# Attention scores of a round's two query blocks issued together, ahead of all four mask products

## The chip, the cores and the metric

The kernel runs on one NeuronCore of a Trainium2 chip. The metric is the device time of one execution in microseconds, lower is better.

## What is computed

Causal self-attention with rotary embedding (2 sequences of 1024 tokens, 1024 channels, 32 heads of 32), a post-norm, a gated feed-forward layer whose weights are looked up in a codebook, and a second post-norm. The part that the change touches is this:

```python
scores = jnp.einsum('bnth,bnsh->bnts', q, k) * (1.0 / math.sqrt(h))
causal = jnp.tril(jnp.ones((T, T), dtype=bool))
scores = jnp.where(causal, scores, -jnp.inf)
attn = jax.nn.softmax(scores, axis=-1)
out = jnp.einsum('bnts,bnsh->bnth', attn, v)
```

## The kernel before

Each engine has its own program, written out by hand in the order in which it runs; semaphores join them. Attention is done in 16 passes (8 groups of 4 heads, 2 sequences) of 8 rounds, 128 rounds in all. A round `u` handles two heads and two query blocks of 128 rows: a short one (`o` = 0) and a long one (`o` = 1), out of the list (0,7), (1,6), (2,5), (3,4), taken in turn. Block number t sees t+1 key blocks, so the two together always have 9, and a short block has 128 to 512 keys and a long one 1024 down to 640. Below, "the (2,5) round" is a round of the third kind.

Rounds are pipelined three deep. In round `u` TensorE (`attention_round`) does, in this order:

1. `scores(i, u, 0)`: the short block's scores for the two heads. The contraction is over 32 rows, so each head's product uses a strip of 32 rows of the array, and the two heads' strips run side by side. Float32 products are recorded as two passes each. Then two mask products (L321 before the change) over all 128 rows: the identity times the triangular mask, in bfloat16, added to the diagonal 128 columns in PSUM. Each raises `scores_done`.
2. `scores(i, u, 1)`: the same for the long block, with keys from 512 on computed in two further strips from the copy `qk_far` (the rows that read `big`), and two mask products.
3. `turn(i, u-1, ...)` (L334): transposes of the previous round's probabilities, in six groups `j` = 0 to 5 (short block: 0 and 1; long block: 2, 3 for the first head, 4, 5 for the second). They alternate between PSUM banks 6 and 7, so group `j` waits until ScalarE has copied out group `j`-2 (`turns_copied`).
4. Between groups 3 and 4, `weigh(i, u-2)` (L353): probabilities times values of the round before that.

`scores(i, u, 0)` waits for the previous round's second exponential and for `o_copied`, the last copy of `weigh(i, u-3)`'s outcome; `scores(i, u, 1)` waits for the previous round's fourth exponential (`exp_done`), since it overwrites the PSUM banks that this one reads.

VectorE in a round: `row_max` 0 and 1 (L922, the maxima of the short block, waiting for `scores_done`), `normalise(u-1, 3)` (L927 reciprocal, L929 scaling), `normalise` 0, `row_max` 2, `normalise` 1, `row_max` 3, two output copies (L937), `normalise` 2.

ScalarE in a round: exponentials 0 and 1 (L629, waiting for the maxima), the copies of turned groups 0 to 3 of the previous round (L638), exponentials 2 and 3, copies 4 and 5. After every fourth round it also issues two loads of queries and keys (L611, L617).

Of the kernel before, what the change touches and what calls it, by code (L numbers as in the profile page):

```python
# [16 lines left out]
P = 128  # L17
# [24 lines left out]
def round_of(u):  # L42

    p, k = divmod(u % ROUNDS, len(BLOCKS))
    return (2 * p, 2 * p + 1), BLOCKS[k]
# [35 lines left out]
def seq_post_ln_layer(nc, x_nat, xT, wqT, wkT, wvT, woT, codebook, entries, idx, codes, cos, sin, ident,  # L81
                      mask, kp, hi_row, sel, out):
    ctx = ExitStack()
    with ctx:
# [186 lines left out]
        def _(pe):  # L271
# [29 lines left out]
            def scores(i, u, o):  # L301

                heads, tbs = round_of(u)
                tb = tbs[o]
                bank, wide, L, d0 = 4 - 4 * o, 1 + o, (tb + 1) * P, tb * P
                if u % 4 == 0:
                    pe.wait_ge((qk_in, far_in)[o][heads[0] // 2], i * 16 + (u // ROUNDS * 16 + 16))
                if not (isinstance(i, int) and i * ROUNDS + u == 0):
                    pe.wait_ge(exp_done, i * STEPS + (4 * u - 2 + 2 * o))
                if o == 0 and not (isinstance(i, int) and i * ROUNDS + u < 3):  # L310
                    pe.wait_ge(o_copied, i * (2 * ROUNDS) + (2 * u - 4))
                for c0 in range(0, L, N):
                    w = min(N, L - c0)
                    for n, hh in enumerate(heads):
                        strip = hh if c0 == 0 else (hh + 2) % HG
                        r = slice(strip * HD, (strip + 1) * HD)
                        qk = qk_sb if c0 == 0 else qk_far
                        mm(ps[:, bank + wide * n + c0 // N, 0:w], qk[r, 0, d0:L], qk[r, 1, c0:c0 + w],
                           start=True, stop=(c0 + w < L))
                for n in range(2):  # L320
                    mm(ps[:, bank + wide * n + d0 // N, d0 % N:d0 % N + P], idb_sb, mask_sb,  # L321
                       start=False, stop=True).then_inc(scores_done, 1)

            def turn(i, u, o, heads=(0, 1)):
                tb = round_of(u)[1][o]
                for n in heads:
                    for c in range(1 + o):
                        j = o * (2 + 2 * n) + (1 - o) * n + c
                        if c == 0:
                            pe.wait_ge(probs_ready, i * STEPS + (4 * u + 2 * o + n + 1))  # L330
                        if not (isinstance(i, int) and i * ROUNDS + u == 0 and j < 2):
                            pe.wait_ge(turns_copied, i * (TURNS * ROUNDS) + (TURNS * u + j - 1))
                        for s in range(4 * c, min(4 * c + 4, tb + 1)):
                            last = nc.tensor.transpose(ps[:, 6 + j % 2, (s % 4) * P:(s % 4 + 1) * P],  # L334
                                                       probs_of[u % 2][2 * o + n][:, s * P:(s + 1) * P], id_sb[:, :])
                        last.then_inc(turns_done, 1)

            def weigh(i, u, free):


                heads, tbs = round_of(u)
                if u % 4 == 0:
                    pe.wait_ge(v_in[heads[0] // 2], i * 16 + (u // ROUNDS * 16 + 16))
                if free:
                    pe.wait_ge(exp_done, i * STEPS + (4 * (u + 2) + 2))
                pe.wait_ge(turns_copied, i * (TURNS * ROUNDS) + (TURNS * u + 6))
                for s in range(tbs[1] + 1):
                    for o in range(2):
                        for n, hh in enumerate(heads):
                            if s <= tbs[o]:  # L350
                                rhs = long_turned[:, u % 2, n, s, :] if o else short_turned[:, u % 2, n, s, :]
                                strip = (hh + 2 * o) % HG
                                last = mm(ps[strip * HD:(strip + 1) * HD, 4 + o, 0:P],  # L353
                                          v_sb[:, hh // 2, s, (hh % 2) * HD:(hh % 2 + 1) * HD], rhs,
                                          start=(s == 0), stop=(s == tbs[o]))
                        if s == tbs[o]:
                            last.then_inc(pv_done, 1)

            def attention_round(i, u, weighed=True, turned=True):

                scores(i, u, 0)
                scores(i, u, 1)
                if turned:
                    turn(i, u - 1, 0)
                    turn(i, u - 1, 1, (0,))
                if weighed:
                    weigh(i, u - 2, True)
                if turned:
                    turn(i, u - 1, 1, (1,))
# [10 lines left out]
            for u in range(2):  # L380
                attention_round(0, u, False, u > 0)
            with pe.Fori(0, PASSES - 1) as i:
                pe.sem_inc(pe_passed, 1)
                for u in range(2, ROUNDS + 2):
                    attention_round(i, u)
            for u in range(2, ROUNDS):
                attention_round(PASSES - 1, u)
# [777 lines left out]
```

## Time and profile before

| | |
|---|---|
| median of 3 runs | 6752.01 us (6750.79 to 6754.25) |
| the profiled execution, own time | 6752.44 us |
| its span (first to last instruction) | 6750.5 us |
| TensorE busy / VectorE / ScalarE / GpSimd | 6615.4 / 4662.0 / 3789.6 / 4927.0 us |
| mean granted TensorE clock | 0.996 of full speed |

The attention rounds fill the stretch from about 680 to 1530 us; before it are the projections, after it the output projection and the feed-forward layer. The profile names engines PE (TensorE products), PEld (its weight loads), DVE (VectorE), ACT (ScalarE), POOL (GpSimd). "L334" is a line of the kernel. Ends of TensorE's products are modelled by the profiler, so distances on TensorE are read below from start to start.

### The profile page before, as it was taken

What the parts mean: (1) busy time and instruction counts of PE and PEld (TensorE: products, weight loads), DVE (VectorE), ACT (ScalarE), POOL (GpSimd) and SP (SyncE); (2) the same over time, 40 slices, a digit from 0 to 9 for tenths busy, and PEclk for the clock granted to TensorE, in tenths of its full rate; (3) what the DMA queues carried; (4) which work ended last, traced back from release to release, by engine and by line L of the source; (5) the groups of instructions that cost most, each with busy time, mean ns of one, the idle gap of its engine ahead of it and who ended that gap; (6) DMA issues with size and microseconds to landing.
All of it is one profiled execution on the core that took longest, in us unless ns stands there. A gap on an engine that the chain in (4) does not pass through costs nothing.

```text
span 6750.5 us, 115830 instructions
## 1 busy us (share of the span) xinstructions
PE 6615.4 (98%) x29584; PEld 4063.9 (60%) x29584; DVE 4662.0 (69%) x11407; ACT 3789.6 (56%) x6692; POOL 4927.0 (73%) x5188
## 2 busy tenths in 40 slices
PE   9999899999999999999999999999999999999998
PEld 3444566666666666666666666666666666666664
DVE  3320888886776876777667776777767777677764
ACT  0000788886666755556555555555556555555552
POOL 7777777777777777777777777777777777777772
PEclk9999999999999999999999999999999999999999
DMA  4232232233333333333333333333333333333331
GB/s 140 64 90 48 56 60 55 58 80 75 82 84 74 78 72 75 65 74 73 73 68 74 76 74 73 67 74 74 72 75 67 73 73 74 74 66 73 73 71 63
DMA packets 479940, 490.59 MB, mean 73 GB/s; under 512 B 228672, under 2 KB 349248, under 8 KB 472896
## 3 DMA queue, kind: packets, MB, share of 16 engines
q10 hardware_dynamic: 298720, 425.47, 22.5%
q0 software_dynamic: 165888, 21.57, 7.8%
q1 hardware_dynamic: 14688, 36.48, 1.4%
q8 instruction: 220, 3.60, 0.2%
q14 instruction: 424, 3.47, 0.2%
HBM read 426.34 MB, written 56.72 MB: 72 GB/s over the span
## 4 chain that ended last, share of the span: by engine, by line
PE 75%; ACT 1%; issue 1%; DVE 0%; DMA 0%; ACTq 0%; DVEq 0%
PE ps L427 42%; PE ps L457 18%; PE ps L476 9%; PE ps L402 3%; PE ps L438 3%; PE ps L444 1%; ACT onehot L771 0%; ACT onehot L775 0%; PE ps L413 0%; PE ps L557 0%; DVE small L1068 0%; ACT arena L866 0%; DMA out_dram<-arena 0%; DVE onehot L1018 0%; DMA arena<-code_low 0%
## 5 line engine op out<-in xcount | busy, mean ns | idle before, releaser
L216 POOL DMA_INDIRECT raw<-in_codebook_dram,idx_sb x5184 | 4926.8, 950 | 1720.6 <-DMA raw<-in_codebook_dram,idx_sb 1566.8
L1018 DVE TENSOR_SCALAR_CACHE_REDUCE onehot<-arena,small 128x512 fp32r<-128x512 f32 x3845 | 2623.4, 743 | 1049.0 <-PE ps L427 998.8
L427 PE MATMUL ps<-onehot,table 128*128 128x512 f32 x12288 | 3267.6, 417 | 23.0 <-ACT onehot L775 18.7
L427 PEld LDWEIGHTS ps<-onehot,table 128*128 128x128 f32 x12288 | 2290.7, 188 | 900.1 <-issue 353.9
L771 ACT ACTIVATE onehot<-arena,small 128x512 fp32r<-128x512 f32 x2307 | 1496.7, 713 | 1139.1 <-PE ps L427 980.1
L775 ACT ACTIVATE onehot<-onehot,small 128x512 fp32r<-128x512 f32 x2307 | 1487.4, 708 | 0.0
L457 PE MATMUL ps<-big,arena 128*128 128x512 f32 x2752 | 1267.9, 597 | 0.0
L457 PEld LDWEIGHTS ps<-big,arena 128*128 128x128 f32 x2752 | 510.2, 189 | 571.7 <-issue 543.7
L1025 DVE SCALAR_TENSOR_TENSOR picked<-arena,small,ps 128x512 f32<-128x512 f16 x768 | 572.3, 745 | 158.3 <-PE ps L438 142.2
L476 PE MATMUL ps<-arena 128*128 128x512 f32 (+1 forms) x1408 | 640.4, 600 | 1.8 <-ACT arena L744 1.2
L922 DVE TENSOR_REDUCE small<-ps 128x1 f32<-128x384 f32 (+7 forms) x512 | 374.2, 752 | 270.1 <-PE ps L321 267.5
L1010 DVE TENSOR_TENSOR big<-ps,big 128x512 f32<-128x512 f32 x704 | 484.9, 691 | 109.8 <-PE ps L476 100.1
L284 PE MATMUL ps<-big,arena 128*128 128x512 f32 x1024 | 442.2, 595 | 16.6 <-DMA big<-in_xT_dram 16.6
L629 ACT ACTIVATE arena<-ps,small 128x384 f32<-128x384 f32 (+7 forms) x512 | 378.1, 745 | 85.9 <-DVE small L922 79.2
L476 PEld LDWEIGHTS ps<-arena 128*128 128x128 f32 (+1 forms) x1408 | 249.0, 190 | 279.8 <-issue 255.1
L334 PE MATMUL ps<-id_sb,arena 128*128 128x128 f32 x2304 | 331.3, 280 | 51.2 <-ACT arena L638 49.4
L638 ACT COPY arena<-ps 128x512 f32<-128x512 f32 (+3 forms) x768 | 330.6, 485 | 65.9 <-PE ps L334 63.8
L284 PEld LDWEIGHTS ps<-big,arena 128*128 128x128 f32 x1024 | 195.4, 191 | 262.6 <-issue 262.6
L1018 DVE DVE_READ_ACCUMULATOR onehot<-arena,small 128x1 f32 x3845 | 321.2, 84 | 0.0
L753 ACT ACTIVATE arena<-ps 128x512 f32<-128x512 f32 (+1 forms) x88 | 52.5, 597 | 467.9 <-PE ps L457 465.1
L334 PEld LDWEIGHTS ps<-id_sb,arena 128*128 128x128 f32 x2304 | 246.6, 141 | 109.2 <-ACT arena L638 74.5
L929 DVE TENSOR_SCALAR arena<-arena,small 128x384 f32<-128x384 f32 (+7 forms) x512 | 276.4, 540 | 18.1
(74 smaller groups left out, 2726.1 us busy)
## 6 DMA issues: line engine op xcount, KB each, us to landing
arena<-code_low ACTq DMA_DIRECT2D x770, 256.0 KB
arena<-code_high ACTq DMA_DIRECT2D x770, 128.0 KB
raw<-in_codebook_dram,idx_sb POOLq DMA_INDIRECT x5184
gathered_units<-raw SPq DMA_DIRECT2D x39, 512.0 KB
arena<-gathered_units ACTq DMA_DIRECT2D x19, 1024.0 KB
queries_keys<-arena ACTq DMA_DIRECT2D x16, 1024.0 KB, 4.0
arena<-queries_keys ACTq DMA_DIRECT2D x32, 512.0 KB
big<-queries_keys ACTq DMA_DIRECT2D x32, 512.0 KB
```

The source lines that it names most:

```text
L216: pool.indirect_dma_start(raw[:, s, n, :], None, codebook, bass.IndirectOffsetOnAxis(ap=idx_sb[:, s, n:n + 1], axis=0), engine_sem=describ ...
L284: last = mm(ps[:, 4 * m + 2 * b + h, :], w_sb[:, m, k, :], big1[:, k, b * T + h * N:b * T + (h + 1) * N], start=(k == 0), stop=(k == KT - 1))
L334: last = nc.tensor.transpose(ps[:, 6 + j % 2, (s % 4) * P:(s % 4 + 1) * P], probs_of[u % 2][2 * o + n][:, s * P:(s + 1) * P], id_sb[:, :])
L427: last = mm(ps[:, 4 + s % 2, :], table[:, k, c, :], onehot[:, k, :], start=(k == 0 and c == 0), stop=(k == KLO - 1 and c == PIECES - 1))
L457: one = mm(ps[:, 2 * (t % 2) + m, :], w_rep[:, m, k, :], big1[:, k, t * N:(t + 1) * N], start=(k == 0), stop=(k == CS - 1))
L476: mm(ps[:, d % banks, :], d_rep[rows, h * P:(h + 1) * P], hT[rows, t * N:(t + 1) * N], start=True, stop=True).then_inc(down_done, 1)
L629: act.activation(probs_of[u % 2][e][:, 0:L], src[:, 0:L], ACT.Exp, bias=negmax[:, e:e + 1], scale=1.0, accum_out=rowsum[:, e:e + 1]).then_ ...
L771: act.activation(onehot[:, k, :], lo_sb[:, s % 2, :], ACT.Abs, bias=kp_sb[:, k:k + 1], scale=-1.0).then_inc(distance_done, 1)
L775: act.activation(onehot[:, k, :], onehot[:, k, :].bitcast(F32), ACT.Relu, bias=one_sb, scale=-1.0).then_inc(near_ready, 1)
L1010: dve.tensor_tensor(big2[:, h, cols], ps[:, d % banks, :], before[:, h, cols], ALU.add).then_inc(y_added, 1)
L1018: dve.tensor_scalar(onehot[:, k, :], lo_sb[:, s % 2, :], kp_sb[:, k:k + 1], None, ALU.is_equal, ALU.add, accum_out=hits[:, k:k + 1]).then_ ...
L1025: dve.scalar_tensor_tensor(picked[:, s % QUAD, :], hi_sb[:, s % 4, :], hi_row_sb, ps[:, 4 + s % 2, :], ALU.is_equal, ALU.mult).then_inc(ma ...
```

## The change

The mask products move out of `scores` into a function of their own, which is called twice after both calls of `scores`.

```diff
                         mm(ps[:, bank + wide * n + c0 // N, 0:w], qk[r, 0, d0:L], qk[r, 1, c0:c0 + w],
                            start=True, stop=(c0 + w < L))
+
+            def mask_diagonal(u, o):
+                d0 = round_of(u)[1][o] * P
+                bank, wide = 4 - 4 * o, 1 + o
                 for n in range(2):
                     mm(ps[:, bank + wide * n + d0 // N, d0 % N:d0 % N + P], idb_sb, mask_sb,
                        start=False, stop=True).then_inc(scores_done, 1)
@@
                 scores(i, u, 0)
                 scores(i, u, 1)
+                mask_diagonal(u, 0)
+                mask_diagonal(u, 1)
                 if turned:
                     turn(i, u - 1, 0)
                     turn(i, u - 1, 1, (0,))
```

No other engine's program changes. TensorE's rows at the head of a (2,5) round, before; L318 are the scores (the short block has 384 keys), L321 the mask products, L334 the transposes:

```order
L311 REGISTER_ALU [waits exp_done]
L318 MATMUL ps<-arena 128x384 [waits o_copied]
L318 MATMUL ps<-arena 128x384
L321 MATMUL ps<-arena 128x128 x2
L309 REGISTER_ALU
L318 MATMUL ps<-arena 128x512 [waits exp_done]
L318 MATMUL ps<-arena 128x512
L318 MATMUL ps<-big 128x256 x2
L321 MATMUL ps<-arena 128x128 x2
L330 REGISTER_ALU
L332 ISA [waits probs_ready]
L334 MATMUL ps<-id_sb,arena 128x128 [waits turns_copied]
```

The same place after the change, where the mask products stand on L325 and the transposes on L338:

```order
L311 REGISTER_ALU [waits exp_done]
L318 MATMUL ps<-arena 128x384 [waits o_copied]
L318 MATMUL ps<-arena 128x384
L309 REGISTER_ALU
L318 MATMUL ps<-arena 128x512 [waits exp_done]
L318 MATMUL ps<-arena 128x512
L318 MATMUL ps<-big 128x256 x2
L325 MATMUL ps<-arena 128x128 x4
L334 REGISTER_ALU
L336 ISA [waits probs_ready]
L338 MATMUL ps<-id_sb,arena 128x128 [waits turns_copied]
```

The short block's two mask products now stand behind the long block's wait for `exp_done` and behind its four score products.

## Rows read from the trace of the kernel before

**Rows 1.** Busy time by stretch: us, busy us (instructions) of PE, PEld, DVE, ACT, POOL, clock, DMA.

```profile
680.00:1530.00 850.00, 786.88 (x8870) 518.96 (x8870) 738.12 (x1786) 701.10 (x1785) 634.47 (x647) 0.99 0.30 61
1530.00:6750.00 5220.00, 5166.50 (x19179) 3252.07 (x19178) 3756.34 (x9437) 3071.07 (x4891) 3787.48 (x4011) 1.00 0.32 73
```

**Rows 2.** The line of the scores: durations in ns, first and last start in us.

```profile
L318 PEld LDWEIGHTS ps<-arena x1024: 181/184/333, 679.9 to 1524.1; 32*128 32x128 f32 x171
```

**Rows 3.** Waits from 680 to 1530 us: total us, times, longest us.

```profile
PEld ps L321 <- issue: 149.9, 224, 1.5
ACT arena L629 <- DVE small L922: 79.2, 104, 5.2
PEld ps L334 <- ACT arena L638: 74.5, 120, 0.9
...
PE ps L334 <- ACT arena L638: 48.2, 125, 0.8
```

**Rows 4.** Timeline of PE, a (2,5) round: start us, us, instruction, count, [idle before].

```profile
1015.72 0.91 PE L318 MATMUL ps<-arena 32*128 32x384 f32 x4 [0.28 <-DVE big L937]
1016.56 0.28 PE L321 MATMUL ps<-arena 128*128 128x128 bf16 x2
1016.78 0.70 PE L318 MATMUL ps<-arena 32*128 32x512 f32 x2
...
1017.84 0.29 PE L321 MATMUL ps<-arena 128*128 128x128 bf16 x2
1017.96 0.61 PE L334 MATMUL ps<-id_sb,arena 128*128 128x128 f32 x4
1018.97 0.98 PE L334 MATMUL ps<-id_sb,arena 128*128 128x128 f32 x7 [0.41 <-ACT arena L638]
```

**Rows 5.** Timeline of DVE, then of ACT, in the same round.

```profile
1016.83 1.02 DVE L922 TENSOR_REDUCE small<-ps 128x1 f32<-128x384 f32 x2 [0.25 <-PE ps L321]
...
1017.42 0.58 ACT L629 ACTIVATE arena<-ps,small 128x384 f32<-128x384 f32 x1 [0.31 <-DVE small L922]
...
1017.99 0.57 ACT L629 ACTIVATE arena<-ps,small 128x384 f32<-128x384 f32 x1
...
1018.55 0.64 ACT L638 COPY arena<-ps 128x256 f32<-128x256 f32 x2
```

**Rows 6.** Timeline of PE, a (0,7) round and the start of the (1,6) round.

```profile
1003.42 0.49 PE L318 MATMUL ps<-arena 32*128 32x128 f32 x4
1003.84 0.28 PE L321 MATMUL ps<-arena 128*128 128x128 bf16 x2
...
1009.43 0.70 PE L318 MATMUL ps<-arena 32*128 32x256 f32 x4
1010.06 0.29 PE L321 MATMUL ps<-arena 128*128 128x128 bf16 x2
```

**Rows 7.** Timeline of ACT in the (0,7) round; ACTq is its queue issuing DMAs.

```profile
1004.22 0.56 ACTq L617 DMA_DIRECT2D big<-queries_keys  x1
1004.90 0.37 ACT L629 ACTIVATE arena<-ps,small 128x128 f32<-128x128 f32 x1 [0.73 <-DVE small L922]
...
1005.89 1.08 ACT L638 COPY arena<-ps 128x512 f32<-128x512 f32 x2 [0.19 <-PE ps L334]
...
1008.97 1.12 ACT L629 ACTIVATE arena<-ps,small 128x1024 f32<-128x1024 f32 x1
1009.97 0.22 ACT L629 ACTIVATION_READ_ACCUMULATOR arena<-ps,small 128x1 f32 x1
```

**Rows 8.** Timeline of DVE in the (0,7) round.

```profile
1004.70 0.60 DVE L929 TENSOR_SCALAR arena<-arena,small 128x640 f32<-128x640 f32 x1
1005.39 0.16 DVE L927 RECIPROCAL small<-small 128x1 f32<-128x1 f32 x1
...
1007.32 1.22 DVE L922 TENSOR_REDUCE small<-ps 128x1 f32<-128x1024 f32 x1
1008.57 0.68 DVE L937 COPY big<-ps 64x128 f32 x2
```

## The prediction, made before the changed kernel ran

> **What bounds the kernel now.** I read the busy time by stretch first. The change touches only the attention stretch; behind it TensorE is busy 5166.5 of 5220 us [rows 1], so nothing there can absorb time that attention loses or pass on more than it gains. In attention TensorE is busy 786.9 of 850 us, VectorE 738.1 and ScalarE 701.1 [rows 1]: three engines close together, so the busy share settles nothing and the waits must. The scores start at 679.9 and last at 1524.1 us [rows 2]; over 127 steps that is 6.65 us a round.
>
> The table of waits [rows 3] shows where TensorE stands still: the transposes (L334) wait for ScalarE's copies (L638), 74.5 us on the load and 48.2 us on the product, some 125 times each, so about once a round. ScalarE's exponentials in turn wait for VectorE's maxima (79.2 us), and these for the mask products. That is a chain that crosses all three engines once a round. One (2,5) round shows it link by link [rows 4, 5]:
>
> - 1016.56 first mask product of the short block
> - 1016.83 VectorE starts the maxima (0.27 later, the product's latency)
> - 1017.42 ScalarE's exponential 0, after 0.31 us of standing idle for the maxima
> - 1017.99 exponential 1
> - 1018.55 copy of turned group 0, with no idle time before it
> - 1018.97 TensorE's group 2, after 0.41 us of idle time
>
> The reader is to see that from the mask product to group 2 there is no slack: each link starts when the one before it is done, and TensorE, at the far end, waits. All the rest of the round (group 3, `weigh`, groups 4 and 5, the next scores) stands behind group 2. So what sets the round is when the short block's mask products are done, and that is what the change postpones.
>
> **The price of the change on TensorE alone.** From the first pass of the short scores to the mask product it is 0.42 us with 128 keys, 0.63 with 256, 0.84 with 384 [rows 4, 6]: 0.21 for each 128 keys and a fixed 0.21. I read the fixed part as the first weight load and the wait for the strips to run empty before the mask product's 128 rows are taken up. From the mask product to the long scores it is 0.22, from the long scores to their mask products 1.06, from there to the first transpose 0.12 for two mask products [rows 4]. Today a (2,5) round takes 2.24 us from 1015.72 to 1017.96. Without the mask products in between, the long scores' passes follow the short ones on the same strips, as second passes follow first ones today, so the fixed 0.21 is hidden: 0.63 (short) + 1.06 (long) + 0.12 + 0.12 (four mask products) = 1.93 to 1.95, about 0.30 less. Over 128 rounds that is 38 us of TensorE's time.
>
> The trace shows a cost at each change between strips and the whole array: the mask products' loads waited 149.9 us, 224 times [rows 3], though most of that is the long streaming itself. The Trainium skill says the same as a rule (TensorEngine Tiling (Array Packing), Key Properties: changing the tiling mode drains TensorE). By that rule alone the change removes one such pair per round and is a gain of the 38 us above; by the chain the gain is not on the path. Both are weighed among the rivals.
>
> **The price on the chain.** The short block's first mask product moves from "short scores + 0.21 + its streaming" to "streaming + 1.06": later by 1.06 - 0.21 = 0.85 us. Bounds: if nothing of the fixed 0.21 is hidden, 1.06; it can't be under 0.85, since the long scores stream for that long. I take 0.85, because a second pass on a strip is what the long scores are like. Behind the moved products are queued VectorE's maxima 0 and 1, and everything that VectorE has behind these; in its program `normalise` stands behind them and can't go ahead. The long block's maxima don't notice: VectorE reaches them about 2 us later than the first ones.
>
> (2,5) and (3,4) rounds, 64 in all, have the pattern of [rows 4, 5]: the whole 0.85 us arrives at group 2. +0.85 each. That transposes 0 and 1 come 0.30 earlier only makes TensorE's wait longer, by 1.15.
>
> (0,7) rounds are different in two ways. ScalarE's exponential 0 is late anyway, because of the loads it issues until 1004.78, and copy 0 waits for the transposes (0.19) [rows 7]. With the maxima starting at 1003.84 + 0.85 + 0.27 = 1004.96, exponential 0 starts at about 1005.29, exponential 1 and copy 0 0.36 later each: 1006.01 against 1005.89, only +0.12. But VectorE then becomes the bound. It had 0.18 us to spare before `normalise` 0 (the scaling that starts at 1004.70 is over, by pace, at 1005.21 and the next starts at 1005.39) [rows 8] and runs without a gap from there to maximum 3 and the output copies. So these come 0.85 - 0.18 = 0.67 later: maximum 3 ends at 1009.20 instead of 1008.53, exponential 3 starts at about 1009.24 instead of 1008.97 (+0.27) [rows 7]. Output copies: 0.67 later, less 0.18 that the second one waits for `weigh` today, plus its time: it ends at about 1009.74, and the next short scores, which need it, start at 1009.77 instead of 1009.43 (+0.34) [rows 6].
>
> (1,6) rounds then meet the wait that the change puts in front of the mask products: the long scores may not start before exponential 3 of the round before is read out. It is read out at 1009.97 + 0.22 = 1010.19 now [rows 7], hence at 1010.46, and the scores can go at 1010.50, though the strips are free at 1009.77 + 0.42 = 1010.19. The mask product comes at 1010.50 + 1.06 = 1011.56 instead of 1010.06 [rows 6]: +1.50 for the (0,7) and (1,6) rounds together. In the other rounds exponential 3 is long done when the strips are free (its round's order is the same, and the short scores stream 0.42 to 0.85 us), so the wait costs nothing there.
>
> **Sum.** 1.50 + 0.85 + 0.85 = 3.20 us for four rounds. 127 rounds have transposes behind the scores, 31.75 times four: 101.6 us. Against the profiled execution, 6752.44 + 101.6 = 6854.0 us. The median of the runs, 6752.01, is 0.4 us from that execution, which makes no difference.
>
> **Bounds.** Low: VectorE and the exponential don't bind in the first two kinds, 0.12 + 3 x 0.85 = 2.67, which is 85 us (6837). High: nothing of the fixed 0.21 is hidden, so 0.21 more in (2,5), in (3,4) and once in the first two: 3.83, which is 122 us (6874). With a few us for the ends: 6832 to 6878.
>
> **The rivals.**
>
> 1. TensorE is the bound, as its busy share says, and the drain saved per round is what counts: 38 us less, 6714 us, faster. For it: 787 of 850 us busy. Against it: TensorE waits for ScalarE about once a round, 0.41 us in [rows 4], and the path that ends that wait has no idle time of its own. It decides from the point where the path from the first mask product to group 2 has more than 0.85 us to spare; today it has none. Chance 0.04.
>
> 2. The copies wait for the transposes in all rounds, as copy 0 does in the (0,7) round [rows 7], rather than for the exponentials. Then each round pays only 0.12 and the sum is 4 x 0.12 x 31.75 = 15 us, 6768 us. Against it: no idle time before copy 0 in the (2,5) round [rows 5]. Chance 0.04, of which 0.02 within the limit of "same".
>
> 3. The new wait binds in all rounds, not in one of four: exponential 3, then the long scores, mask products, maxima, exponentials, copies and exponential 3 again is a closed loop. If each round pays as the (1,6) round does, 1.50 - 0.34 = 1.16, the sum is 4 x 1.16 x 31.75 = 147 us, 6900 us. For it: three engines at over 80%. Against it: the exponential of a (0,7) round is the longest (1024 keys) and the short scores behind it are nearly the shortest. Chance 0.08.
>
> That the change doesn't do what it says I rule out: TensorE's rows stand in the program in the new order in every round.
>
> **How the numbers follow.** My forecast, with its bounds, 0.84; rival 1 0.04; rival 2 0.04; rival 3 0.08. The predicted time is the forecast's, 6854 us. The range from 6832 to 6878 leaves out the three rivals. About 0.2% (13.5 us) is what a measurement of this kernel can tell from no change: faster 0.04, same 0.02, slower 0.94.
>
> **What would show it.** Right: the attention stretch about 100 us longer and the stretches around it as long as before; TensorE busy in it no more than before, with its waits for ScalarE's copies more than doubled (some 1 us a round more); VectorE's first maxima waiting for the mask products in every round; the step from one round's first scores to the next's longer by about 0.34, 1.16, 0.85 and 0.85 us from (0,7) to (3,4). Wrong, toward rival 1: the same waits as today and a stretch of about 806 us. Wrong, toward rival 3: the long scores waiting for the exponential in all rounds.

## The result and the profile after

The changed kernel takes 6887.3 us (median of 6 runs, 6877.6 to 6895.1) against 6754.3 us for the kernel before (6 runs beside it): a ratio of 1.0198, 95% interval 1.0186 to 1.0209, or 133 us more. The forecast was 102 us more, 6854 us in a range from 6832 to 6878. So the sign and three quarters of the size came out, and the time lies above the range. The profiled execution took 6895.1 us with a span of 6893.3 us, 142.8 us over the span before.

First where the time went. Busy time by stretch of the changed kernel, with the columns of [rows 1]; the last three figures are the granted clock, the DMA share and GB/s:

```profile
680.00:1673.00 993.00, 796.16 (x8832) 550.12 (x8833) 734.63 (x1782) 696.85 (x1780) 736.16 (x750) 0.94 0.27 53
1673.00:6893.00 5220.00, 5166.98 (x19221) 3256.56 (x19220) 3758.32 (x9441) 3073.07 (x4897) 3690.69 (x3909) 1.00 0.32 73
```

What follows attention is as long as before: a stretch of 5220 us holds 5167.0 us of TensorE's work against 5166.5 [rows 1], and from the last round's first scores to the end it is 5226.6 us against 5227.8. The attention stretch has grown from 850 to 993 us, all of the difference. In it VectorE and ScalarE do the work of before; TensorE's is 9 us more, and its granted clock has gone from 0.99 to 0.94. The prediction has no term for that.

The waits between 680 and 1673 us, to be laid beside [rows 3]:

```profile
DVE small L928 <- PE ps L325: 391.4, 127, 226.7
...
PEld ps L338 <- ACT arena L644: 188.6, 120, 2.0
ACT arena L635 <- DVE small L928: 186.1, 137, 11.4
PE ps L338 <- ACT arena L644: 166.6, 125, 1.8
PEld ps L325 <- issue: 98.8, 128, 1.5
```

The first row is VectorE's maxima waiting for the mask products, once a round (226.7 us of it is one wait ahead of the first round). TensorE's waits for ScalarE's copies have gone from 74.5 and 48.2 us to 188.6 and 166.6 us, still about once a round; the one wait of the mask products' loads is left where there were two. The timeline of PE shows a (2,5) round and the (3,4) round after it, the counterpart of [rows 4]:

```profile
890.74 0.92 PE L318 MATMUL ps<-arena 32*128 32x384 f32 x4 [0.19 <-DVE big L943]
...
892.44 0.40 PE L325 MATMUL ps<-arena 128*128 128x128 bf16 x4
892.68 0.61 PE L338 MATMUL ps<-id_sb,arena 128*128 128x128 f32 x4
894.85 0.98 PE L338 MATMUL ps<-id_sb,arena 128*128 128x128 f32 x7 [1.57 <-ACT arena L644]
895.77 1.95 PE L357 MATMUL ps<-arena 128*32 128x128 f32 x36
...
898.56 0.70 PE L318 MATMUL ps<-arena 32*128 32x512 f32 x2
...
900.48 0.40 PE L325 MATMUL ps<-arena 128*128 128x128 bf16 x4
...
903.34 1.54 PE L338 MATMUL ps<-id_sb,arena 128*128 128x128 f32 x6 [1.80 <-ACT arena L644]
904.81 2.62 PE L357 MATMUL ps<-arena 128*32 128x128 f32 x36
...
908.17 0.38 PE L318 MATMUL ps<-arena 32*128 32x128 f32 x2
```

From the first scores to the mask products of the (2,5) round it is 1.70 us where it was 0.84: 0.86 later, forecast 0.85. From the first scores to the first transpose it is 1.94 us where it was 2.24: the 0.30 us that TensorE saves is there too, and stands as idle time (1.57 us instead of 0.41) in front of the next transposes. The step from this round to the next is 7.82 us, 0.86 more than the 6.96 us before (1015.72 to 1022.68, where the next round's first scores stand).

The (3,4) round is something else. Its six transposes after the wait take 1.54 us and its 36 products 2.62 us, where the kernel before needs 0.87 and 1.74 for the same:

```profile
1022.68 1.13 PE L318 MATMUL ps<-arena 32*128 32x512 f32 x4
...
1026.61 0.87 PE L334 MATMUL ps<-id_sb,arena 128*128 128x128 f32 x6 [0.64 <-ACT arena L638]
1027.41 1.74 PE L353 MATMUL ps<-arena 128*32 128x128 f32 x36
```

The busy time of the changed kernel in that stretch, with the granted clock as the third figure from the end:

```profile
903.40:906.80 3.40, 3.40 (x34) 2.86 (x36) 2.26 (x5) 2.58 (x7) 2.48 (x4) 0.52 0.06 3
```

TensorE stood idle for 1.80 us, and as it takes up work again it runs at the lower of its two levels, 1.2 GHz, for 3.4 us; that makes this round's step 9.61 us instead of 8.05. The Trainium skill (TensorE: Matmul & The Clock Gate, Terms) gives the penalty of such a stretch as half of its length, which makes an estimate of 1.7 us here. The trace agrees roughly: the two entries are 0.67 and 0.88 us longer, 1.55 together.

Read over the whole trace, 25 of the steps between rounds from the second round on are such slow ones (22 after (3,4), 3 after (2,5) rounds). One of the three is not a fall after a wait: it begins at 704.2 us, in the low stretch at the start of attention, which ends at 708.7 us here and at 697.5 us in the kernel before. The 25 are 39 us longer in all than quick steps of the same kind. The quick steps average 6.50, 7.15, 7.82 and 8.05 us from (0,7) on, against 6.01, 6.12, 6.97 and 7.20 before: 3.22 us more in four rounds, forecast 3.20. 31.75 times 3.22 is 102 us, and 102 + 39 = 141 of the 142.8 us between the spans.

### The profile page after: what moved, and what is told of

Same layout as the page of the kernel before. It is cut to its first block, busy times and chain, and to the rows that moved or that the text cites. A ratio compares the mean times of both kernels' runs of the same rounds, so it can differ in the third digit from the quotient of the medians.

```text
span 6893.3 us, 115830 instructions
## 1 busy us (share of the span) xinstructions
PE 6625.6 (96%) x29584; PEld 4100.0 (59%) x29584; DVE 4660.4 (68%) x11407; ACT 3787.4 (55%) x6692; POOL 4933.0 (72%) x5188
## 4 chain that ended last, share of the span: by engine, by line
PE 74%; ACT 1%; issue 1%; DVE 0%; DMA 0%; ACTq 0%; DVEq 0%
PE ps L433 41%; PE ps L463 17%; PE ps L482 9%; PE ps L408 3%; PE ps L444 3%; PE ps L450 1%; ACT onehot L777 0%; PE ps L419 0%; ACT onehot L781 0%; PE ps L563 0%; DVE small L1074 0%; DVE onehot L1024 0%; ACT arena L872 0%; DMA out_dram<-arena 0%; DMA arena<-code_low 0%
## 5 line engine op out<-in xcount | busy, mean ns | idle before, releaser
L1031 DVE SCALAR_TENSOR_TENSOR picked<-arena,small,ps 128x512 f32<-128x512 f16 x768 | 572.2, 745 | 157.8 <-PE ps L444 142.8
L338 PE MATMUL ps<-id_sb,arena 128*128 128x128 f32 x2304 | 346.6, 289 | 171.6 <-ACT arena L644 167.8
L338 PEld LDWEIGHTS ps<-id_sb,arena 128*128 128x128 f32 x2304 | 257.5, 146 | 230.3 <-ACT arena L644 188.6
```

The lines of the kernel that those rows point to most:

```text
L1031: dve.scalar_tensor_tensor(picked[:, s % QUAD, :], hi_sb[:, s % 4, :], hi_row_sb, ps[:, 4 + s % 2, :], ALU.is_equal, ALU.mult).then_inc(ma ...
```

## The experiments

Two theories stood against each other. **Chain and clock**: the chain over VectorE and ScalarE costs 3.2 us in four rounds as forecast, and the longer waits also cost TensorE its clock. **Chain alone, mis-sized**: the missing 31 us are a dearer chain. A "fall" below is a fall of the granted clock to the lower level. Steps given below for an experiment are read from the starts in its timeline, in the steady part of attention.

### The change in two kinds of rounds only

```diff
                 scores(i, u, 0)
+                if u % 4 in (0, 1):
+                    mask_diagonal(u, 0)
                 scores(i, u, 1)
-                mask_diagonal(u, 0)
+                if u % 4 not in (0, 1):
+                    mask_diagonal(u, 0)
                 mask_diagonal(u, 1)
```

This is e1_late_kinds; e2_early_kinds has (2, 3) in both places.

> The changed order is used in the (2,5) and (3,4) rounds only; the other two kinds keep the order of before. Theory (chain price as in the prediction, plus TensorE clock falls to half speed after the long waits): the chain costs 0.85 us in each of 64 rounds, 54 us over before; on top of it some clock falls of about 1.6 us each in the (3,4) rounds, between 0 and 30 us in all, since these rounds keep their wait of 2 us. So 6808 to 6840 us. Rival (the 33 us missing in the prediction were a mis-sized chain price in these two kinds): the rounds without a fall of the clock take over 7.9 and 8.2 us instead of 7.82 and 8.05.

> The changed order is used in the (0,7) and (1,6) rounds only. Theory: +1.50 us for each pair of them (0.34 and 1.16), 32 pairs, 48 us over before, hence 6802 us, and no falls of the clock in the middle of the attention rounds, because the waits that remain are 1.6 us and less. Rival (the chain price of this pair is mis-sized): more than 6815 or less than 6790 us with the clock at full speed.

Measured: e1 6849.5 us (4 runs) and e2 6796.1 us (4 runs) against 6751.3 us (13 runs): ratios 1.0147 (1.0130 to 1.0164) and 1.0067 (1.0050 to 1.0084), or 98 and 45 us more. Busy time from 720 to 1500 us, of e1 and then of e2:

```profile
720.00:1500.00 780.00, 675.81 (x7459) 465.26 (x7457) 618.13 (x1489) 584.67 (x1490) 582.50 (x596) 0.95 0.27 52
```

```profile
720.00:1500.00 780.00, 684.68 (x7877) 456.76 (x7874) 645.58 (x1579) 617.71 (x1580) 580.42 (x590) 1.00 0.28 55
```

e2, the clock at 1.00, is the chain price of the first two kinds by itself: steps of 6.39 and 7.15 us, 1.41 together over before, forecast 1.50; 32 pairs make 45 us, which is what was measured. That the two agree to the microsecond is luck: in this trace it is 50 us more from the first round to the last, a longer stretch at the low clock at the start included, and 6 us less behind them. (What follows the last round's start takes 5221 to 5228 us in these traces, e4's apart.) e1's quick steps are 7.83 and 8.06 us, 0.86 each over before, as forecast, and its clock is at 0.95. It has 26 slow steps (18 in the (3,4) and 8 in the (2,5) rounds), 42 us in all, so 54 + 42 = 96 of the 98 us. The theory's form held, but I had given the falls 0 to 30 us, and the time lies above the expected range: there are as many as in the changed kernel, though half of the rounds keep their short waits. So how often the clock falls can't be summed from the kinds: 98 + 45 is 143, and the changed kernel pays 133.

### The wait filled with work

```diff
+                        if j == 1:
+                            for _ in range((10, 12, 15, 0)[u % 4]):
+                                nc.tensor.transpose(ps[:, 7, 0:P], id_sb[:, :], id_sb[:, :])
                         for s in range(4 * c, min(4 * c + 4, tb + 1)):
```

> The changed kernel, with 10, 12 and 15 extra transposes of the identity (about 0.11 us each) ahead of transpose group 1 in the (1,6), (2,5) and (3,4) rounds, where TensorE stands waiting for ScalarE's copy anyway; their outcome is overwritten by group 1. Theory: they cost nothing on the chain, keep TensorE at work, and the granted clock stays at full speed from the second pass on; what is left is the chain price of 102 us, 6854 to 6862 us, 25 to 33 us faster than the changed kernel. Rival (the missing 33 us are chain, not clock): 6887 us or more, as TensorE's extra work can only lengthen a chain.

Measured: 6855.0 us (4 runs), ratio to before 1.0154 (1.0137 to 1.0170). That is 104 us over the kernel before beside it, where the changed kernel is 133 us over its own: 29 us less, though TensorE has 1184 transposes more to do. The timeline of PE in a (3,4) round; L339 are the added transposes:

```profile
1010.67 0.40 PE L325 MATMUL ps<-arena 128*128 128x128 bf16 x4
1010.90 0.50 PE L341 MATMUL ps<-id_sb,arena 128*128 128x128 f32 x3
1011.24 1.80 PE L339 MATMUL ps<-id_sb 128*128 128x128 f32 x15
...
1013.53 0.88 PE L341 MATMUL ps<-id_sb,arena 128*128 128x128 f32 x6 [0.17 <-ACT arena L647]
1014.34 1.74 PE L360 MATMUL ps<-arena 128*32 128x128 f32 x36
```

and its busy time from 720 to 1500 us:

```profile
720.00:1500.00 780.00, 730.76 (x8348) 537.71 (x8345) 608.76 (x1476) 579.25 (x1477) 579.70 (x592) 1.00 0.27 52
```

Group 2 starts 2.86 us after the mask products, as in the changed kernel (900.48 to 903.34), so the chain is untouched; the wait before it is 0.17 us, the transposes are back at 0.88 and the products at 1.74, the clock at 1.00, and no step is slow past the first rounds. 6855 us is the forecast's 6854: what the forecast lacked is the clock. (That the two agree to the microsecond is chance: the steps are 6.56, 7.16, 7.83 and 8.06 us, 3.3 us more in four rounds, and in this trace it is 107 us more from the first round to the last and 6 us less behind them.) "Chain alone" has fallen.

### The wait of one kind filled

```diff
-                            for _ in range((10, 12, 15, 0)[u % 4]):
+                            for _ in range((0, 0, 15, 0)[u % 4]):
```

> The changed kernel with the 15 extra transposes in the wait of the (3,4) rounds only; (1,6) and (2,5) rounds keep their waits of 1.6 and 1.8 us. Theory: most falls of the clock came at the end of the (3,4) rounds' wait of 2.07 us (19 of 27 such rounds in the profile against 1 of 27 for (2,5)); with that wait filled nearly all of them are gone, 6855 to 6865 us. Rival (the clock falls for the waits of all rounds taken together, whichever is filled): some falls move to the (2,5) rounds, and the time lies between 6865 and 6887 us.

> The kernel of e7_fill_34_only again, beside runs of before without the stalls. The profile of e7 had no slow (3,4) round but nine falls of the clock in its steady part. If a fall belongs to the (3,4) rounds' wait: 6853 to 6860 us. If falls move to the (2,5) rounds once the (3,4) rounds are filled: 6862 to 6882 us, with 7 to 18 slow (2,5) rounds in the profile.

These runs, and e5, e6, e8, e9, e10 and e13, fell on three chips on which the kernel before itself took 13,210 us: engines stood for thousands of us without a cause that the profile shows, before attention and in its first 18 rounds or so, while the other rounds run undisturbed. In every one of these traces the disturbed rounds end within some 20 us of GpSimd's last gather (7252 to 7261 us), so the undisturbed ones run without gathers beside them. The kernel before was not profiled there. So only differences count here, and above all the steps of the undisturbed rounds. Measured: 110 us over before both times, ratios 1.0084 (1.0068 to 1.0099) and 1.0082 (1.0067 to 1.0098). The timeline of PE of e11, a (2,5) and a (3,4) round:

```profile
7607.27 0.61 PE L341 MATMUL ps<-id_sb,arena 128*128 128x128 f32 x4
7609.44 1.55 PE L341 MATMUL ps<-id_sb,arena 128*128 128x128 f32 x7 [1.57 <-ACT arena L647]
7610.92 3.00 PE L360 MATMUL ps<-arena 128*32 128x128 f32 x36
...
7617.25 1.80 PE L339 MATMUL ps<-id_sb 128*128 128x128 f32 x15
...
7619.55 0.88 PE L341 MATMUL ps<-id_sb,arena 128*128 128x128 f32 x6 [0.17 <-ACT arena L647]
```

No (3,4) round is slow any more, and eight (2,5) rounds are (nine in e7), after a wait of 1.57 us that in the changed kernel cost nothing except twice. The rival was right: the falls moved. In the last 108 rounds, the undisturbed ones, the changed kernel has 20 falls, so filling one kind took away rather more than half of them, not nearly all; the eight cost 13 us. The time alone would not have told: 110 us over before is 6861 us on the undisturbed chip, inside e7's range for the theory and a microsecond under e11's for the rival, and it holds what the 15 transposes cost in the disturbed (3,4) rounds (217 to 242 us each, where e5 has 199 at most).

### The maxima taken off the path

These two kernels leave out the row maxima, with 0 in their place, and the exponentials wait for the mask products directly.

```diff
-                act.wait_ge(negmax_done, i * STEPS + (4 * u + e + 1))
+                act.wait_ge(scores_done, i * STEPS + (4 * u + e + 1))
+                act.wait_ge(rinv_done, i * STEPS + (4 * u + e - 3))
...
-                row_max(i, u, 0)
-                row_max(i, u, 1)
```

and so for `row_max` 2 and 3; the first `rinv_done` wait only from the second round on. e5 has TensorE's order of before, e6 the changed one.

> The order of before; the row maxima are left out and the exponentials take 0 in their place, so they wait for the mask products directly. This leaves out part of the computation. Theory: the link from the mask product to exponential 0 gets shorter by the maximum's 0.3 to 0.7 us a round, but copy 0 then waits for the transposes instead, so only part of it shows: 20 to 45 us faster than before, 6706 to 6732 us. It stands here for the comparison with the next run.

> The changed order, with the row maxima left out as in the run before it. Theory (the price is what the mask products' delay of 0.85 us exceeds the slack ahead of copy 0): the link freed by the maxima is slack that absorbs some of the delay, so the price against the run before it falls from 102 us to 40 to 65 us of chain, with few or no falls of the clock as the waits are shorter. Rival (the price is the exchange of instructions on TensorE itself, or the clock, and has nothing to do with the path over VectorE): the difference stays at 100 us or more.

Measured: e5 20 us under before (13189.1 against 13209.6; 0.9985, 0.9976 to 0.9994), e6 20 us over it (13229.2; 1.0015, 1.0006 to 1.0025): the changed order costs 40 us instead of 102 plus the falls. The steps are 6.00, 5.94, 6.81, 6.80 and 5.78, 6.65, 7.27, 7.33 us: 1.48 us more in four rounds instead of 3.22, with no fall of the clock in the undisturbed rounds. PE, group 0 and group 2 of a (2,5) round, in e5 and in e6:

```profile
7501.76 0.61 PE L334 MATMUL ps<-id_sb,arena 128*128 128x128 f32 x4
7502.61 0.98 PE L334 MATMUL ps<-id_sb,arena 128*128 128x128 f32 x7 [0.24 <-ACT arena L642]
```

```profile
7515.38 0.60 PE L338 MATMUL ps<-id_sb,arena 128*128 128x128 f32 x4
7516.96 0.98 PE L338 MATMUL ps<-id_sb,arena 128*128 128x128 f32 x7 [0.98 <-ACT arena L648]
```

ScalarE's last reading of exponential 1 and copy 0 in the same rounds, in e5 and in e6:

```profile
7501.85 0.25 ACT L633 ACTIVATION_READ_ACCUMULATOR arena<-ps,small 128x1 f32 x1
7502.19 0.65 ACT L642 COPY arena<-ps 128x256 f32<-128x256 f32 x2
```

```profile
7516.45 0.20 ACT L639 ACTIVATION_READ_ACCUMULATOR arena<-ps,small 128x1 f32 x1
7516.54 0.64 ACT L648 COPY arena<-ps 128x256 f32<-128x256 f32 x2
```

With the maxima off the path, the path from the mask product to copy 0 has slack in e5: copy 0 comes 0.34 us after the reading starts instead of 0.09, since it waits for the transposes (from 7501.76), and group 2's wait is down from 0.41 to 0.24. That slack absorbs a part of the delay. In the (0,7) round, where copy 0 waits for the transposes in the kernel before already [rows 7], the changed order is even quicker (5.78 against 6.00): I read that as a part of TensorE's 0.30 us paid out. So the price hangs on the path over VectorE, not on the exchange of instructions.

### The mask product ahead of the short scores

```diff
+                if o == 0:
+                    for n in range(2):
+                        mm(ps[:, bank + n, d0:L], idb_sb, mask_sb, start=True, stop=False)
+                    for a, z in ((d0, L), (0, d0))[:1 + (d0 > 0)]:
+                        for n, hh in enumerate(heads):
+                            r = slice(hh * HD, (hh + 1) * HD)
+                            last = mm(ps[:, bank + n, a:z], qk_sb[r, 0, d0:L], qk_sb[r, 1, a:z],
+                                      start=(a == 0 and d0 > 0), stop=True)
+                            if a == 0:
+                                last.then_inc(scores_done, 1)
+                    return
...
-                mask_diagonal(u, 0)
                 mask_diagonal(u, 1)
```

> The short block's two mask products come first in the round, as the first writers of their banks, and the short scores are added to them (the diagonal 128 keys first, the rest of the block in a product of its own); then the long scores and their two mask products. So TensorE takes up the row strips once a round, as in the changed kernel, but the short scores are complete before the long ones start. Theory (what costs is only that the maxima of the short block wait behind the long scores): the price of 133 us is gone, and time lies within 20 us of before, 6734 to 6756 us, as the chain is 0 to 0.15 us shorter a round. Rival (taking up the strips once a round is itself dear, by a slower start of the long scores or by waits for exponential 3): 6790 us or more.

Measured: 6758.1 us (10 runs) against 6751.3: 1.0007 (0.9998 to 1.0017), no difference that counts, 2 us above what was expected. PE in a (2,5) round; L314 and L336 are the mask products, L318 the short scores, L329 the long ones, L349 the transposes:

```profile
1014.58 0.28 PE L314 MATMUL ps<-arena 128*128 128x128 bf16 x2 [0.20 <-DVE big L953]
1014.79 0.71 PE L318 MATMUL ps<-arena 32*128 32x128 f32 x6
...
1016.51 0.28 PE L336 MATMUL ps<-arena 128*128 128x128 bf16 x2
1016.63 0.61 PE L349 MATMUL ps<-id_sb,arena 128*128 128x128 f32 x4
1017.89 0.98 PE L349 MATMUL ps<-id_sb,arena 128*128 128x128 f32 x7 [0.66 <-ACT arena L654]
```

TensorE takes up the strips once a round here too, and the first transpose comes 2.05 us after the round's start instead of 2.24. The price of 133 us is gone, since the short scores are complete ahead of the long ones on their strips. What is saved on TensorE is spent waiting (0.66 us before group 2 instead of 0.41). The steps are 5.85, 6.16, 6.94, 7.15 us, 0.2 less in four rounds, and from the first round to the last it is 838.1 us instead of 842.9. Those 5 us are lost again in the feed-forward layer of the profiled execution, as two lines of the waits from 6320 to 6345 us show:

```profile
ACT onehot L787 <- SPq L243: 15.6, 1, 15.6
...
PE ps L443 <- ACT onehot L791: 10.2, 1, 10.2
```

ScalarE waits 15.6 us for the store of gathered weights (L243), a wait that no trace of before, of the changed kernel, or of e1, e2 and e3 has. GpSimd's last gather starts at 6655 us here and at 6647 us in the trace before, and attention is over 5 us sooner: what follows attention has come closer to the gathers by both. That a quicker attention runs into them is a reading of this one trace.

### Copies ahead of exponential 1

```diff
                     exponent(i, u, 0)
-                    exponent(i, u, 1)
                 if turned:
-                    for j in range(4):
-                        copy_turned(i, u - 1, j)
+                    copy_turned(i, u - 1, 0)
+                    copy_turned(i, u - 1, 1)
+                if scored:
+                    exponent(i, u, 1)
+                if turned:
+                    copy_turned(i, u - 1, 2)
+                    copy_turned(i, u - 1, 3)
```

e8, e9 and e13 have this and the mask product first; e10 has it alone, with TensorE as before. (e12, the same kernel as e13, gave no time.)

> As e4_mask_first, and ScalarE does the copies of turned groups 0 and 1 between exponentials 0 and 1 instead of behind both. Theory: with the strips taken up once a round the transposes of groups 0 and 1 are done 0.3 us earlier than before, early enough that these copies fit ahead of exponential 1, so that group 2 waits for one exponential less; the time saved on TensorE becomes of use: 10 to 25 us faster than before, 6727 to 6742 us. Rival (the transposes are not done when exponential 0 ends, so exponential 1 and all behind it only come later): 6755 us or more.

> The kernel of e8_mask_first_copies_early again. In its profile the steps from one round's scores to the next's are 6.03, 6.12, 6.45 and 6.78 us against 6.01, 6.12, 6.97 and 7.20 before, 0.92 less in four rounds or 29 us over 127, while all times on that chip were twice as long through stalls outside the steady rounds. If the rounds are what counts: 6722 to 6735 us. Rival (stalls hid a loss elsewhere): 6745 us or more.

> The order of TensorE as before; only ScalarE's copies of groups 0 and 1 go between exponentials 0 and 1. Theory (the gain of the run before needs the earlier transposes that taking up the strips once a round gives): the copies wait for the transposes, exponential 1 and all behind it come later by about what group 2 gains, and the time is within 12 us of before, 6740 to 6764 us. Rival (the copies' place alone makes the gain): 6735 us or less.

> The same kernel once more, for a comparison with before on a chip without the long stalls of the last two jobs. If the steps between rounds decide (29 us less in the attention rounds): 6720 to 6735 us. If something behind the attention rounds gives part of it back, as in e4_mask_first: 6735 to 6745 us.

Measured: 20, 19 and 18 us under before (ratios 0.9985, 0.9986 and 0.9987; intervals from 0.9975 to 0.9996), and for e10 3 us under it (0.9997, 0.9988 to 1.0007), no difference. ScalarE and then PE in a (2,5) round of e9:

```profile
7506.47 0.58 ACT L645 ACTIVATE arena<-ps,small 128x384 f32<-128x384 f32 x1 [0.24 <-DVE small L942]
...
7507.18 0.65 ACT L654 COPY arena<-ps 128x256 f32<-128x256 f32 x2
```

```profile
7506.76 0.61 PE L349 MATMUL ps<-id_sb,arena 128*128 128x128 f32 x4
7507.61 0.98 PE L349 MATMUL ps<-id_sb,arena 128*128 128x128 f32 x7 [0.24 <-ACT arena L654]
```

Copy 0 now stands behind one exponential, and group 2's wait has shrunk to 0.24 us. The steps are 5.98, 6.13, 6.52, 6.76 us, 0.92 less than before in four rounds. e10's are 6.20, 6.07, 6.81, 7.06, 0.18 less. So the once-a-round strips are worth something after all, when what waits behind them is moved as well. The full 29 us weren't seen, as some 18 rounds are disturbed on those chips. From the 21st round's start to the last one's it is 679 us in all three traces, against 703 in the trace before and 699 in e10's: 24 us less in 107 rounds. What an undisturbed chip gives stays open, and e4's wait for the gathers speaks for less than 29 us: on the disturbed chips they were over by about 7260 us, before attention was done.

## Why the prediction was wrong, point by point

- **What bounds attention**: right. The chain from the mask product over maxima, exponentials and copy to group 2 sets the round; e5 and e6 show that the price falls when a link of it is taken out.
- **TensorE's own saving of 0.30 us a round**: right in size (2.24 to 1.94) and right in that it is worth nothing (idle time before group 2). Rival 1 fell. (Its stretch of "about 806 us" should read 812, 850 less 38; nothing hangs on it.)
- **0.85 us on the chain in (2,5) and (3,4) rounds**: right, 0.85 and 0.85, and 0.86 each in e1. The upper bound of 1.06 wasn't needed.
- **0.34 and 1.16 in (0,7) and (1,6) rounds**: 0.49 and 1.03 in the changed kernel, 0.38 and 1.03 in e2; the two errors nearly cancel, so that the sum of 1.52 against 1.50 is in part luck. Why the (0,7) steps vary (6.31 to 6.68 us in these traces) isn't shown. For the mechanism, a (0,7) and the start of the (1,6) round behind it in the changed kernel: VectorE's maxima wait 1.18 us in the (0,7) round, exponential 3 is read out at 915.16, and the mask products come 1.78 us after the first scores, forecast 1.79.

```profile
909.72 0.49 DVE L928 TENSOR_REDUCE small<-ps 128x1 f32<-128x128 f32 x2 [1.18 <-PE ps L325]
```

```profile
914.97 0.19 ACT L635 ACTIVATION_READ_ACCUMULATOR arena<-ps,small 128x1 f32 x1
```

```profile
914.49 1.42 PE L318 MATMUL ps<-arena 32*128 32x256 f32 x6
...
916.27 0.40 PE L325 MATMUL ps<-arena 128*128 128x128 bf16 x4
```

- **The new wait for exponential 3 "costs nothing" in the other rounds**: right in price, not in the reason. Exponential 3 isn't long done in the (2,5) rounds: there the loads of the long scores wait for it too, 31 times, by 0.26 us on average, as they do in the (1,6) rounds. But the mask products of the (2,5) round still come 1.70 us after the first scores, forecast 1.69.
- **The sum of the chain, 101.6 us**: right; e3, the same kernel with its clock kept up, is 104 us over before.
- **The wait made longer costs nothing more**: this is the step that failed. The prediction says that transposes which come earlier "only make TensorE's wait longer, by 1.15", and prices that at nothing; its page of before showed a clock of 0.99 and 1.00 [rows 1], and no rival had the clock fall. It costs 39 us in the profiled execution and about 31 in the median of the runs, 25 stretches of 3.4 us at 1.2 GHz, each paid with about 1.6 us.
- **The other signs**: the stretches around attention are unchanged, as forecast. Rival 3 (paying for exponential 3 in all rounds) didn't come: its price would be 1.16 a round, and only the (1,6) round pays near that. So although 6887 us is nearer to rival 3's 6900 than to 6854, its mechanism is not what was missing.

What remains open: which waits bring a fall about. 1.80 us of idle time in the (3,4) rounds mostly did, 1.57 us in the (2,5) rounds seldom in the changed kernel, eight times in e1 and in eight of some 27 rounds once the (3,4) rounds were filled. With the (1,6) rounds' 1.3 us as the longest (e2) there was none from 720 to 1500 us. The runs show that the kinds depend on each other, not by what rule.

## What to carry to other kernels

Before a product is moved behind others to spare TensorE a change between strips and the whole array, look who waits for it: here 0.30 us saved a round was bought with 0.85 us on a path without slack. Where a change makes TensorE's idle time longer, price the clock as well: the idle stretch is paid, and then the work behind it at half speed. When several engines share a loop, moving one engine's instructions pays only together with the others' order: mask first, or copies early, alone gave nothing that could be measured; both together took 19 us off, on the disturbed chips.

## What the runs showed of the hardware

- The granted clock fell after waits of 1.57 and 1.80 us, in rounds that have such a wait each time. The kernel before, with idle times of 0.24 to 0.64 us before group 2, kept 1.00 from 720 us on, and so did e4 with up to 0.89 and e2 with about 1.3 us in the (1,6) rounds, both read from 720 to 1500 us.
- Work that nobody needs, put into a wait, made the kernel 29 us faster (e3), with the clock at 1.00 instead of 0.96 from 720 to 1500 us.
- Products on strips that are free started ahead of those that stand before them in the program and wait for their strip. In a (0,7) round of the changed kernel the long block's far products (on the other two strips, reading `big`) start at 908.20, 0.03 us after the short scores' first pass at 908.17 (shown above) and before their second at 908.38:

```profile
908.20 0.70 PE L318 MATMUL ps<-big 32*128 32x512 f32 x2
908.38 0.71 PE L318 MATMUL ps<-arena 32*128 32x128 f32 x4
```

The near products, on the short scores' strips, still set the end, so the first transpose came no sooner than forecast.
